# First transfers in halves on two queues, four high products first in the shared expert, and a filled wait with the output bias on ScalarE at the end

## The reference

```
x = x + x @ W_base.T + b_base + 2 * sum_e cond[b,e] * (x @ As[e].T) @ Bs[e].T      # layer 0
x = x + x @ (sum_g cond[b,g] * weight[g] * mask).T + bias                          # layer 1
rw = softmax(cond); the two largest of each batch, normed to sum 1                 # layer 2
x = x + sum over the two chosen experts w * (gelu(x@gate[e]) * (x@up[e])) @ down[e]
      + (gelu(x@shared_gate) * (x@shared_up)) @ shared_down
e = argmax(cond[b])                                                                # layer 3
x = x + (silu(x@W_up[e].T + b_up[e]) * (x@W_gate[e].T + b_gate[e])) @ W_down[e].T + b_down[e]
```

## Time and profile before

| | us |
|---|---|
| median of 3 runs | 88.13 |
| lowest, highest | 86.94, 89.66 |
| the profiled execution | 87.69 |
| its span, from the first to the last instruction | 85.9 |

### The profile page before, as it was taken

One profiled execution on the slowest core, in us unless ns is written; L12 is line 12 of the kernel. 1 busy time (PEld: TensorE's weight loads), 2 busy tenths in 40 slices (PEclk: granted clock), 3 DMA queues, 4 the chain that ended last, 5 costly groups with the idle time before them and its releaser, 6 DMA issues.

```text
span 85.9 us, 1918 instructions
## 1 busy us (share of the span) xinstructions
PE 82.2 (96%) x618; PEld 77.3 (90%) x618; DVE 47.3 (55%) x109; ACT 30.7 (36%) x55; POOL 15.6 (18%) x20
## 2 busy tenths in 40 slices
PE   6899999999999999999999999999999999999980
PEld 6788977888888999999999999999999999999970
DVE  0278769743534998329328438446365564563270
ACT  4332692877556420221221221222302402407320
POOL 3020396097666900000000000000000000000000
PEclk9999999999999999999999999999999999999999
DMA  2996006889960000686889889989998979726102
GB/s 12 349 418 256 0 0 183 303 296 402 404 241 10 0 0 4 197 268 272 229 301 342 255 265 346 275 291 331 265 313 309 306 262 323 273 72 154 60 0 61
DMA packets 5479, 18.57 MB, mean 216 GB/s; under 512 B 608, under 2 KB 1888, under 8 KB 5472
## 3 DMA queue, kind: packets, MB, share of 16 engines
q1 hardware_dynamic: 5040, 17.49, 59.9%
q10 hardware_dynamic: 432, 0.98, 2.9%
HBM read 17.95 MB, written 0.52 MB: 215 GB/s over the span
## 4 chain that ended last, share of the span: by engine, by line
PE 87%; DMA 4%; POOL 3%; DVE 2%; issue 1%; DVEq 0%
PE bank L661 33%; PE bank L671 17%; PE bank L684 9%; PE bank L698 4%; PE bank L632 4%; PE bank L641 4%; PE bank L633 4%; DMA first_sb<-in_first 4%; PE bank L581 3%; POOL shared_l L245 3%; PE bank L570 2%; PE bank L649 2%; PE bank L648 2%; PE bank L651 2%; DVE p L377 1%
## 5 line engine op out<-in xcount | busy, mean ns | idle before, releaser
L661 PE MATMUL bank<-x_t,pair_w 128*128 128x128 f32 (+1 forms) x256 | 31.3, 275 | 0.0
L661 PEld LDWEIGHTS bank<-x_t,pair_w 128*128 128x128 f32 x256 | 30.0, 192 | 0.3
L296 ACT ACTIVATE gelu<-bank 128x512 f32<-128x512 f32 x24 | 14.2, 596 | 32.8 <-PE bank L661 28.0
L463 DVE SCALAR_TENSOR_TENSOR hid<-gelu,wsel,bank 128x512 f32<-128x512 f32 x16 | 12.0, 748 | 18.7 <-PE bank L661 18.6
L671 PE MATMUL bank<-hid,pair_w 128*128 128x128 f32 x128 | 16.9, 275 | 0.0
L671 PEld LDWEIGHTS bank<-hid,pair_w 128*128 128x128 f32 x128 | 15.6, 192 | 0.1
L259 POOL TENSOR_TENSOR hid_l<-hid,hid_h 128x512 fp32r<-128x512 f32 x8 | 10.2, 1291 | 4.9 <-ACT hid_h L319 4.9
L461 DVE TENSOR_TENSOR hid<-gelu,bank 128x512 f32<-128x512 f32 x8 | 5.5, 688 | 6.7 <-ACT gelu L296 4.3
L684 PE MATMUL bank<-x_t,w 128*128 128x128 f32 x64 | 8.7, 276 | 0.0
L684 PEld LDWEIGHTS bank<-x_t,w 128*128 128x128 f32 x64 | 7.9, 192 | 0.2 <-issue 0.2
L632 PE MATMUL bank<-x_h,shared_h 128*128 128x512 f32 x16 | 6.4, 401 | 0.1
(11 more groups left out here) (68 smaller groups left out, 74.7 us busy)
## 6 DMA issues: line engine op xcount, KB each, us to landing
pair_w<-in_skill SPq DMA_DIRECT2D x16, 768.0 KB, 5.5
w<-in_layer SPq DMA_DIRECT2D x8, 384.0 KB, 5.2
rest_sb<-in_rest SPq DMA_DIRECT2D x1, 533.0 KB, 4.0
x_t<-in_x SPq DMA_DIRECT2D x1, 512.0 KB, 4.8
shared_sb<-in_shared ACTq DMA_DIRECT2D x1, 512.0 KB, 4.0
out_x<-out_sb SPq DMA_DIRECT2D x8, 64.0 KB, 4.2
shared_sb<-in_shared ACTq DMA_DIRECT2D x1, 256.0 KB, 4.3
first_sb<-in_first ACTq DMA_DIRECT2D x1, 192.0 KB, 3.2
```

What stands on the lines that cost most here:

```text
L296: act.activation(gelu[:, n, :], ps[:, :], ACT.Gelu_apprx_tanh).then_inc(gelu_ready, 1)
L463: dve.scalar_tensor_tensor(hid[:, n, :], gelu[:, n, :], wsel[:, bass.DynSlice(weight, 1)], u_ps[n][:, :], ALU.mult, ALU.mult).then_inc(hid ...
L661: mm = pe.matmul(ps[:, S * t:S * (t + 1)], pair_w[:, slot, n, 128 * t:128 * (t + 1)], x2_t[:, columns(b)], start=True, stop=True)
```

## The change

The first two loads are each cut into partitions 0 to 63, issued by SP, and 64 to 127, issued by ACT; both `first` halves come ahead of the `head` halves. The waits for `first_in` and `head_in` go from 16 to 32. In the shared expert `shared_high` keeps only the high by high product, and a new `shared_middle` has the low weights by high `x`; for k = 0 and 1 four highs come first, then four middles, then four lows; from k = 2 on the order of the products is as before. At the end of TensorE's program, of the two up products of batch 6 only the first stays ahead of `down(B-1, 1, 1)`; the second comes behind it, after a wait for the first SiLU (both write the same bank, which ACT reads). `silu_step` waits for its own chunk alone. For the last two batches ACT adds the output bias to `x3_t` into a new buffer `x3b`, behind its last SiLUs, and DVE's last step is a `tensor_tensor` of the product and `x3b`, without the bias operand.

```diff
-            sp.dma_start(head_sb[:, :], head[:, :]).then_inc(head_in, 16)
+            sp.dma_start(first_sb[0:64, :], first[0:64, :]).then_inc(first_in, 16)
+            sp.dma_start(head_sb[0:64, :], head[0:64, :]).then_inc(head_in, 16)
             sp.dma_start(rest_sb[:, :], rest_in[:, :]).then_inc(rest_landed, 16)
...
-            act.dma_start(first_sb[:, :], first[:, :]).then_inc(first_in, 16)
+            act.dma_start(first_sb[64:128, :], first[64:128, :]).then_inc(first_in, 16)
+            act.dma_start(head_sb[64:128, :], head[64:128, :]).then_inc(head_in, 16)
             act.preload_act_table(ACT.Exp)
-            act.wait_ge(head_in, 16)
+            act.wait_ge(head_in, 32)
...
-                    act.wait_ge(up3_done, HC * b + (c + 1 if is_last(b) else HC))
+                    act.wait_ge(up3_done, HC * b + c + 1)
...
+            def add_bias3(b, q):
+
+                act.wait_ge(x3_ready, b + 1)
+                act.activation(x3b[:, q, :], x3_t[:, q, :], ACT.Identity, bias=bsel[:, 2 * HC, b:b + 1]).then_inc(x3b_ready, 1)
...
             silu_step(B - 1, 1)
+            add_bias3(B - 2, 0)
+            add_bias3(B - 1, 1)
...
-            dve.wait_ge(head_in, 16)
+            dve.wait_ge(head_in, 32)
...
+            def result_sum(b, q):
+
+                dve.wait_ge(x3b_ready, b - (B - 2) + 1)
+                dve.wait_ge(stored[q], 16 * (fills(b, q) - 1))
+                dve.wait_ge(out_done, b + 1)
+                dve.tensor_tensor(out_sb[:, q, :], out_bank(b)[:, 0:S], x3b[:, q, :], ALU.add).then_inc(out_ready, 1)
...
-            result(B - 2, 0)
-            result(B - 1, 1)
+            result_sum(B - 2, 0)
+            result_sum(B - 1, 1)
...
-            pe.wait_ge(first_in, 16)
+            pe.wait_ge(first_in, 32)
             mix1_part(0, EARLY)
-            pe.wait_ge(head_in, 16)
+            pe.wait_ge(head_in, 32)
...
                 if k == 0:
                     pe.wait_ge(sh_high, m + 1)
+                pe.matmul(ps[:, :], shared_h[:, m, 128 * t:128 * (t + 1)], x2_h[:, N * h:N * (h + 1)], start=True, stop=False)
+
+            def shared_middle(k, m):
+
+                h, t = k // T, k % T
+                ps, _ = shared_ps(k, m)
+                if k == 0:
                     pe.wait_ge(sh_low, m + 1)
-                high = x2_h[:, N * h:N * (h + 1)]
-                pe.matmul(ps[:, :], shared_h[:, m, 128 * t:128 * (t + 1)], high, start=True, stop=False)
-                pe.matmul(ps[:, :], shared_l[:, m, 128 * t:128 * (t + 1)], high, start=False, stop=False)
+                pe.matmul(ps[:, :], shared_l[:, m, 128 * t:128 * (t + 1)], x2_h[:, N * h:N * (h + 1)], start=False, stop=False)
...
             shared_high(1, 1)
+            shared_middle(0, 0)
+            shared_middle(0, 1)
+            shared_middle(1, 0)
+            shared_middle(1, 1)
             shared_low(0, 0)
...
-            both_chunks3(B - 2, 0, 0)
+            product3(B - 2, 0, 0, 0)
             down(B - 1, 1, 1)
+            pe.wait_ge(silu3_ready, 1)
+            product3(B - 2, 0, 0, 1)
             both_chunks3(B - 2, 0, 1)
```

More of the change, by code:

```diff
@@ L104, in build @@
         x3_t = sb("x3_t", [C, 2, S])
+        x3b = sb("x3b", [C, 2, S])
         silu3 = sb("silu3", [128, 2, HC, S])
@@ L147, in build @@
             sem("up3_done"), sem("gate3_done"), sem("half3_ready"), sem("tanh3_ready"), sem("gate3_ready"), sem("hid3_ready"))
-        silu3_ready = sem("silu3_ready")
+        silu3_ready, x3b_ready = sem("silu3_ready"), sem("x3b_ready")
         out_done, out_ready = sem("out_done"), sem("out_ready")
@@ L723, in _ @@
             for k in range(2, NSH):
-                for part in (shared_high, shared_low):
-                    for m in range(2):
-                        part(k, m)
+                for m in range(2):
+                    shared_high(k, m)
+                    shared_middle(k, m)
+                for m in range(2):
+                    shared_low(k, m)
                 if k >= 3:
```

## The result

| | us | executions |
|---|---|---|
| before, median | 87.62 (86.94 to 90.13) | 22 |
| after, median | 88.16 (87.68 to 91.65) | 22 |
| ratio | 1.0061 [1.0037, 1.0086] | |
| the profiled execution after | 88.08, span 86.3 | 1 |

The change costs 0.6%, some 0.5 us; the prediction had a gain of 0.5 us.

The account below looks back on a forecast made before the run. TensorE's matmuls, busy 96% of the span, were taken to bound the kernel, so gains lay only where PE was unfed. Start and shared expert 0.36 plus end 0.16 made 0.52 us: from 87.91 to 87.4, range 86.4 to 88.5.

Parts of the forecast that it names:

- part 1: Kernel start: first two loads in halves on both queues; PE's first product 0.44 us earlier, of which 0.22 stays.
- term of +0.22: Kernel start: gain kept from the earlier first product, since 0.44 us at half clock speed is worth 0.22.
- 3.55 predicted: Kernel start: time at which PE could take its first product, 0.44 us earlier than 3.99.
- Rival (a): Kernel start: the start buys nothing, `first` is no earlier; 0.30 us gained in all, 87.6; chance 0.2.
- lower bound: Kernel start: least gain in PE's first product, 0, if halves land as late as wholes; upper bound 0.5 us.
- worth nothing: Kernel start: value of cutting the loads by the Trainium skill's rule, since disjoint partition halves share the same DMA engines.
- Part 2: Shared expert: four high products first, third released by DVE at 12.83 instead of POOL at 12.97; 0.14 us gained.
- Part 3: Kernel end: 0.10 us from the moved up product plus 0.06 from bias on ScalarE, 0.16 gained.
- PE's new stall: Kernel end: `down(B-1,1)`, reached sooner, waits for its `hid`; a new stall of 0.11 us.
- rival (d): Kernel end: Identity brings a table load, with 1.28 us the change is 0.41 slower, 88.3; chance 0.05.
- rival (b): Kernel end: `hid` wait and DVE's shifted work take the moved product's gain, 0.06 left there; 87.5; chance 0.15.
- rival (c): Kernel start: the clock rises as much earlier as the work, 0.22 us more gained; 87.2; chance 0.1.

Follow-up runs that it names:

- first_halved: The kernel after, with only `first` in halves by partitions and `head` whole on SP's queue behind its half: 88.43 us, ratio 1.0109 [1.0048, 1.017].
- start_only: The kernel before with only the first two loads cut into partition halves on both queues: 89.24 us, ratio 1.010 [1.0043, 1.0157].
- rest_halves: no_start with `rest` in halves by partitions, both on SP's queue: median 89.18 us over four executions, ratio 1.0225 [1.014, 1.031].
- x_halves: no_start with `x` in halves by partitions, both on SP's queue: median 88.78 us over four executions, one of them 292.79.
- no_start: The kernel after with the first two transfers whole again, one on each queue: 87.14 us, ratio 0.9933 [0.9896, 0.9969] against before.
- swapped: no_start with the queues exchanged, `first` whole on SP and `head` whole on ACT: 86.97 us, ratio 0.993 [0.9885, 0.9975].
- waits_first: no_start with DVE's wait for PE's product put first of the three waits ahead of its last add: 86.98 us, ratio 0.9946 [0.9902, 0.999].
- head_first: The kernel after with `head` in halves first on both queues and `first` whole behind ACT's half: median 91.11 us.
- columns: The kernel after with halves cut by columns, each with all 128 partitions: 88.33 us, ratio 1.0106 [1.0048, 1.0165].
- preload_first: The kernel after with ACT's first table load ahead of its two transfers: median 90.35 us over four executions, 87.60 to 91.67.
- x_after_first: first_halved with `x` issued only when `first` has landed, at most four transfers under way: 91.35 us, ratio 1.0413 [1.0264, 1.0563].
- shared_early: no_start with the shared expert's load issued right behind `first`, five whole transfers at once: 87.4 us, ratio 1.001 [0.9959, 1.0062].
- end_only: The kernel before with only the end changed, the moved up product and the output bias on ScalarE: 87.3 us, ratio 0.9972 [0.9925, 1.0018].

## Why the prediction was wrong

**The step that failed** is part 1, and in it three sentences: "Each queue issues one transfer more before the next, 0.4 us", "`head` where the pair ends now, 3.8 to 3.95", and "since the engines are full `rest` should hardly be later". Measured: 0.58 and 0.84 us for SP's two halves, and 0.60 for the whole transfer behind them; `head` at 4.57 to 6.10; `rest` at 6.23 in after and 7.99 in first_halved, 1.0 and 2.8 later than before (5.21). I took a fixed rate of 0.43 MB/us and reordered bytes under it. The rate was not fixed: it fell to 223 GB/s with the DMA share still near 1. The term of +0.22 gained became -0.81 in the profiled execution, and 1.0% [0.43, 1.57] lost in start_only.

**What was left out** is the shared expert's load. I listed `rest`, `x` and ACT's table load as what moves, but ACT issues that load too, behind its work on `head`, and its rounding stands ahead of its bias. In the trace of before it landed at about 7.8, 1.6 us before PE's product asked for the bias (9.42), and in after at 9.69: 1.0 of slack by the late issue and the long transfer gone, and ACT blocked for 0.56.

**What held in part 1**: PE's first product at 3.46, near the 3.55 predicted. Where the halves of `first` head the queues they land between 3.35 and 3.82; whole at the head of a queue, `first` landed between 3.83 and 4.60, but at 3.61 and 3.62 in rest_halves and x_halves. So the step from bytes to landing was about right for the transfer in front, and wrong for all behind it. Rival (a) had the right place, but its price was nothing where a loss was due: no case of mine let part 1 lose. The lower bound "0 (the halves land as late as the wholes)" was no lower bound. The Trainium skill's rule (DMA: Bandwidth & Descriptors, Rules for kernel authors), by which such transfers are left whole, pointed the right way; the runs here show more than the "worth nothing" that I drew from it, a loss.

**Part 2** was right in mechanism and nearly in size: DVE's second write releases the third product, 0.18 to 0.19 for the predicted 0.14. That it takes part 1's shift along held too, with the sign turned: 0.81 late became 0.63 late.

**Part 3**: the moved product gained 0.15 to 0.16 for 0.10; PE's new stall in the last `down` was 0.05 (0.94 us in the chain against 0.89), where I took 0.11. There was no table load between the last SiLU and the Identity (ACT's SiLUs run from 82.04, its biases from 82.56), so rival (d) is out; rival (b) is out because the moved product did gain. The 0.06 of the shorter add did come but was spent on the order of the waits, a cost that I had put at nothing. Together 0.11 for 0.16.

**The clock**, rival (c): the trace of after still has the four records of `first` at half pace, 1.22 us, starting 0.53 earlier than before. Then PE stood still for `head` until 5.16, and the next records follow at full pace: the second of layer 0's mix 0.29 us behind the first, where before it was 0.41; start_only, whose clock had risen by then, has 0.29 there too. So the half-speed stretch did not end at 5.42 as I had said, but before, while PE had nothing to do. Whether it ended as much earlier as the work, this trace can't show, and there was nothing to gain from it. Nor is the time of the rise fixed; see the last section.

The prediction's sum was 0.22 + 0.14 + 0.16 = 0.52 gained. In the profiles it was 0.81 lost, 0.18 and 0.11 gained, 0.17 gained by chance and 0.01 on the way: 0.81 - 0.18 - 0.01 - 0.17 - 0.11 = 0.34, and the 0.05 left of the 0.39 lies outside these steps. The time measured lies on the other side of no change, within the range given.

## What to carry to other kernels

Leave the loads of a start whole until a trace shows that cutting them pays: here, in the one trace of each kernel, every cut of a load into halves, by partitions or by columns, on one queue or two, went with one to four microseconds at a third to three quarters of the rate, and all but one of the traces of whole transfers kept it. A loss of time is measured for halves of the first loads, not for those of `rest` and `x`. Before cutting or moving a load, list all transfers that its engine issues later, and for each of them the first instruction that waits for it, in its engine's own order, since an engine that waits for a late load also blocks what stands behind it. In a row of waits ahead of the last instruction, put first the one that is satisfied last (some 0.1 us here).

The best versions run here have parts 2 and 3 with whole transfers: no_start with 0.9933 [0.9896, 0.9969] of the kernel before, and swapped (0.993) and waits_first (0.9946), which can't be told from it.

## What the runs showed of the hardware that I had not expected

**Halves and the rate.** Busy DMA engines are not engines at their rate: in the windows of 1 us from 3 to 6, kernels of whole transfers moved 378 to 434 GB/s at a share near 1, and those with halves had two or three such windows of 124 to 334, at shares of 0.76 to 1.18 (head_first only one, 208 at 0.65). One execution of whole transfers is an exception: the profiled one of waits_first (90.05 us for a median of 86.98) had 302 from 3 to 4, then 422 and 400. So a low rate can come without halves; it did in one such trace of nine. The runs exclude the partitions of a half (columns), the queue (swapped, rest_halves), the table load (preload_first) and the number of transfers under way (x_after_first, shared_early). Not run were halves that raise a semaphore each (both halves of a load raised the same one), cuts into other sizes, and cuts of a load that is alone. Why a cut load has this effect on those around it is left open, and so is how the same stretch varies between executions, since each kernel has one trace.

**Issue time.** At the start, an issue of 128 partitions took 0.33 to 0.47 us in the kernels with no cut by partitions, whole or by columns. One of 64 partitions took 0.56 to 0.88, the whole transfer behind it up to 0.60, and one of the shared expert's loads, whole, still 0.91 in first_halved.

**The clock's rise differs between executions of the same start.** The kernels end_only and no_start have the same start. Their timelines, end_only first:

```profile
3.88 1.22 PE L596 MATMUL bank<-first_sb 128*128 128x128 f32 x4 [0.21 <-DMA first_sb<-in_first]
```

```profile
3.92 0.71 PE L596 MATMUL bank<-first_sb 128*128 128x128 f32 x4 [0.26 <-DMA first_sb<-in_first]
```

The same four records take 1.22 us in one execution and 0.71 in the other, with nearly the same landing (3.83 and 3.87), and layer 1's product on `x` starts at 10.63 and 9.52. The granted clock column is 1.00 in every row of both, so the rise is read from the pace of the records. It can come later still. The chain of waits_first, whose start is again that of no_start:

```profile
5.87 3.41 PE bank L585 x6
9.28 1.86 PE bank L596 x12
```

No_start takes 1.72 and 1.34 us for these. A difference of 1 us and more between executions of one start is larger than the whole effect studied, so the steps above compare before and after only because in both traces the four records are at half pace (1.23 and 1.22).

**A halved clock after a wait.** In two traces the granted clock fell back to 0.50 for over three microseconds: in head_first after PE had stood still for 2.45 us, in x_after_first after 2.62, each time about a microsecond after it had taken up work again. A late transfer can so cost more than the wait.

**The order of waits.** DVE's last add stands behind three waits. With the one for PE's last product standing last, the add began 0.12 us after that product (end_only); with it standing first, 0.02 after it (waits_first).
